# Building a graph's adjacency from a list of the pairs that hold edges, in place of four passes over all edge turns

## The reference

```python
dst = jnp.minimum((512 * jax.random.uniform(..., (16384,)) ** 2.0).astype(jnp.int32), 8191)
_o = jnp.argsort(dst, stable=True)          # the edges come sorted by destination
src, dst = src[_o], dst[_o]
A = A.at[src, dst].add(edge_weight)         # layer 0: weighted adjacency, then normalised
h = leaky_relu((A_norm @ h @ W_gcn[l] + b) @ W_mlp[l] + b)      # two rounds
# layer 1: four blocks of attention over the edges (edge counts)
# layer 2: adjacency of 0 and 1, made symmetric, three diffusion steps
# layer 3: two relations (edge_type 0 and 1), weights mixed from 30 bases:
w = jnp.einsum('rb,bio->rio', att, basis)   # basis is 30 x 512 x 512, per layer
```

## Time and profile before

| | |
|---|---|
| median of 3 runs | 1030.19 us (1028.79 to 1030.89) |
| the profiled execution: its own time | 1028.4 us |
| its span, first to last instruction | 1026.6 us |
| PE busy | 902.5 us, 88% of the span, 4358 instructions |
| DVE busy | 562.3 us, 55% |
| ACT busy | 429.2 us, 42% |
| POOL busy | 207.8 us, 20% |
| mean granted TensorE clock | 0.927 of full |
| adjacency: first opening of a bank to last closing | 12.7 to 188.6 us |

### The profile page before, as it was taken

One profiled execution on the slowest core, in us unless ns is written; L12 is line 12 of the kernel. 1 busy time (PEld: TensorE's weight loads), 2 busy tenths in 40 slices (PEclk: granted clock), 3 DMA queues, 4 the chain that ended last, 5 costly groups with the idle time before them and its releaser, 6 DMA issues.

```text
span 1026.6 us, 15204 instructions
## 1 busy us (share of the span) xinstructions
PE 902.5 (88%) x4358; PEld 685.6 (67%) x4359; DVE 562.3 (55%) x1236; ACT 429.2 (42%) x702; POOL 207.8 (20%) x147
## 2 busy tenths in 40 slices
PE   5878778799967999989999999999999796699998
PEld 4544354466745786967877778777878464678877
DVE  6845565885667545555565554664546847420110
ACT  4845465452332575236732477224662131221110
POOL 3000000230244012430133311332112322012100
PEclk9886986799987999999999999999999899599899
DMA  6727365445245444363454533552446653020100
GB/s 182 173 64 159 69 138 134 90 144 133 48 132 144 108 131 104 114 158 88 131 116 153 110 98 117 152 163 60 128 125 158 192 159 71 1 82 0 41 11 31
DMA packets 40920, 113.18 MB, mean 110 GB/s; under 512 B 9040, under 2 KB 9552, under 8 KB 33204
## 3 DMA queue, kind: packets, MB, share of 16 engines
q1 hardware_dynamic: 22116, 75.88, 31.3%
q10 hardware_dynamic: 18768, 36.83, 10.4%
HBM read 105.35 MB, written 7.34 MB: 110 GB/s over the span
## 4 chain that ended last, share of the span: by engine, by line
PE 71%; DVE 14%; issue 8%; ACT 4%; DVEq 2%; POOL 1%; ACTq 0%; DMA 0%
PE ring L1534 33%; PE ring L1772 21%; PE ring L1599 9%; PE ring L1552 5%; PE mix_ps L1563 1%; DVE stats L1018 1%; DVE yp L1327 1%; ACT yp L855 1%; PE mix_ps L1622 1%; DVE xl L1344 1%; ACT yp L886 1%; DVE yp L1332 1%; DVE y L1027 1%; DVE ohd L1143 1%; DVE mv L1021 1%
## 5 line engine op out<-in xcount | busy, mean ns | idle before, releaser
L632 POOL TENSOR_TENSOR wl<-wraw,wh 128x2048 fp32r<-128x2048 f32 x35 | 160.8, 4599 | 398.6 <-ACT wh L694 398.6
L1599 PE MATMUL ring<-ohs,ohd 128*128 128x512 f32 x368 | 101.0, 437 | 20.2 <-DVE ohs L1155 16.9
L1599 PEld LDWEIGHTS ring<-ohs,ohd 128*128 128x128 f32 x368 | 77.5, 215 | 49.4 <-DVE ohs L1155 26.3
L1143 DVE SCALAR_TENSOR_TENSOR ohd<-iota,dstT,vals 128x256 fp32r x184 | 79.7, 478 | 31.9 <-issue 26.0
L636 POOL TENSOR_TENSOR rstd<-ve,half 128x1 f32<-128x1 f32 x52 | 29.8, 576 | 291.2 <-DVE ve L1023 291.2
L737 ACT ACTIVATE ohs<-iota,minus_srcT 128x512 fp32r<-128x512 f32 x80 | 56.1, 716 | 45.3 <-PE ring L1599 20.7
L694 ACT ACTIVATE wh<-wraw 128x2048 fp32r<-128x2048 f32 x35 | 66.6, 1905 | 4.9 <-DMA wraw<-in_L_gnn_root 4.9
L1005 DVE TENSOR_TENSOR qk_l<-ring,qk_h 128x512 fp32r<-128x512 f32 x32 | 21.7, 690 | 75.8 <-ACT qk_h L719 75.8
L719 ACT ACTIVATE yT_h<-ring 128x512 fp32r<-128x512 f32 x32 | 19.1, 597 | 100.9 <-PE ring L1552 100.9
L1563 PE MATMUL mix_ps<-quad,att_shift 120*32 120x512 f32 x384 | 52.7, 634 | 3.3 <-ACT mixed L709 3.3
L1005 DVE TENSOR_TENSOR PT_l<-ring,PT_h 128x512 fp32r<-128x512 f32 x64 | 39.6, 681 | 19.6 <-ACT PT_h L719 19.6
(11 more groups left out here) (337 smaller groups left out, 2253.9 us busy)
## 6 DMA issues: line engine op xcount, KB each, us to landing
quad<-in_L_gnn_basis SPq DMA_DIRECT2D x60, 960.0 KB, 7.9
wraw<-in_L_gnn_m_w ACTq DMA_DIRECT2D x8, 1024.0 KB, 5.4
mix_scratch<-mixed SPq DMA_DIRECT2D x128, 32.0 KB, 1.8
wraw<-in_L_gnn_wv ACTq DMA_DIRECT2D x4, 1024.0 KB, 5.3
wraw<-in_L_gnn_wq ACTq DMA_DIRECT2D x4, 1024.0 KB, 5.2
wraw<-in_L_gnn_wk ACTq DMA_DIRECT2D x4, 1024.0 KB, 5.4
wraw<-in_L_gnn_wo ACTq DMA_DIRECT2D x4, 1024.0 KB, 5.4
wraw<-mix_scratch ACTq DMA_DIRECT2D x4, 1024.0 KB, 5.7
```

The lines of the kernel that those rows point to most:

```text
L632: g.tensor_tensor(wl[s][:], wraw[s][:], wh[s][:].bitcast(F32), ALU.subtract).then_inc(weight_lo, 1)
L1143: return v.scalar_tensor_tensor(out, at.unsqueeze(1).broadcast_to([P, 4, HALF]), dstT[:, e], vals[:, e, :].rearrange("p a b -> p (a b)").u ...
L1599: last = te.matmul(ring[:, bass.ds(banks[2 * r + j], 1), :], marks, ohs[:, u, :], start=False, stop=False)
```

## The change

The adjacency is no longer built in passes. On the chip a list is made of the pairs (turn, half) that hold edges, ordered by half, and one loop goes along it. `BODY` becomes 4, so a turn is 512 edges and there are 32; a pair is called a **unit**. The slots stay 8 (two units).

- **The list.** TensorE sums the flags of turns and halves (`unit_hit`), multiplies with triangles of ones for each unit's rank and whether it is the first of its half, and places codes of 6 bits, four to a word, in `words`. The chain is VectorE, TensorE, VectorE, TensorE, VectorE, about 20 short operations, on POOL's new constants (`upto`, `upto_half`, `unit_scale`); the 16 small `pow2` fills go.
- **The loop.** Each engine reads a word per four units (`value_load`), shifts out the turn and the "first of a half" bit, and does four tiles. The first 32 units are unconditional; behind them come up to 8 and then more, each behind a test of the count.
- **At a first unit** TensorE closes the two banks of the half before, opens two others, and ScalarE and VectorE move the closed half out after they made their tiles of the new unit.
- **Mixing.** One group stands ahead of every second unit (`j % 2 == 0`), starting ahead of unit 0; 16 groups in 32 units.
- **CT.** `CT[0] = Csum - CT[1]` moves from the end of each pass to the loop over H (round 0), behind each low part, and SP waits for these (`ct_ready`).
- **Norm.** The four `xn0` of VectorE become four operations on one column (`nmean`), and ScalarE computes `Relu(rstd * x + nmean)`.

```diff
-BODY = 8
-SPAN = 4
+BODY = 4
 TURNS = ET // BODY
-SLOTS = BODY
+SLOTS = 2 * BODY
-ACT_OF_ONE = (1, 3, 5, 7)
-ACT_OF_BOTH = (0, 2, 4, 6, 7)
+SURE = TURNS
+NEXT = SURE + 2 * WORD
+ACT_OF = (1, 3)
+EVICTS = 2
@@ SP
                 if g == 20:
-                    sp.wait_ge(pass_dve, DVE_EVICTS * (SETS_HELD + NT))
+                    sp.wait_ge(ct_ready, NT)
@@ ScalarE
+            def unit(i, j, word):
+                turn = act.snap((word >> (BITS * j)) & (TURNS - 1))
+                first = act.snap((word >> (BITS * j + BITS - 1)) & 1)
+                source_tiles(j % 2 * BODY, i * BODY, turn)
+                act.reg_add(half_no, half_no, first)
+                with act.If(first > 0):
+                    ...
+                    act.wait_ge(half_ready, done)
+                    evict(m, 0 or 1)
...
-                a.activation(xn0[:, t, :], xn0[:, t, :], ACT.Relu).then_inc(h0_hi, 1)
+                a.activation(xn0[:, t, :], x[:, t, :], ACT.Relu, bias=nmean[:, t:t + 1], scale=rstd[:, t:t + 1]).then_inc(h0_hi, 1)
@@ VectorE
+            def unit(i, j, word):
+                turn = dve.snap((word >> (BITS * j)) & (TURNS - 1))
+                first = dve.snap((word >> (BITS * j + BITS - 1)) & 1)
+                dve.reg_add(half_no, half_no, first)
+                half = dve.snap(half_no, min_val=0, max_val=HALVES - 1)
                 for u in range(BODY):
+                    s = j % 2 * BODY + u
+                    e = bass.ds(turn * BODY + u, 1)
+                    dve.wait_ge(onehot_used, i * BODY + (u + 1))
+                    ins = destination(half, s, e)
+                    if u not in ACT_OF:
+                        ins = v.tensor_scalar(ohs[:, s, :], iota[:], srcT[:, e], None, ALU.is_equal)
                     ins.then_inc(dst_ready, 1)
...
-                normalise(xn0[:, t, :], x[:, t, :], t, t)
+                dve.wait_ge(ln_rstd, t + 1)
+                v.scalar_tensor_tensor(nmean[:, t:t + 1], mv[:, t, 0:1], -1.0, rstd[:, t:t + 1], ALU.mult, ALU.mult).then_inc(ln_xn, 1)
...
                 v.tensor_tensor(hb_l[1][:, t, :], hv[:, t % 2, :], f(hb_h[1][:, t, :]), ALU.subtract).then_inc(tile_taken, 1)
+                v.tensor_tensor(CT[0][:, t, :], Csum[:, t, :], CT[1][:, t, :], ALU.subtract).then_inc(ct_ready, 1)
@@ TensorE
+            def unit(i, j, word):
+                first = pe.snap((word >> (BITS * j + BITS - 1)) & 1)
+                with pe.If(first > 0):
+                    done = pe.snap(half_no, min_val=0, max_val=HALVES - 1)
+                    ...
+                    zero(old[0], False)
+                    pe.wait_ge(half_act, done * EVICTS + EVICTS)
+                    zero(old[1], False).then_inc(half_ready, 1)
+                    pe.wait_ge(half_dve, done * EVICTS + EVICTS)
+                    zero(new[0], True)
+                    zero(new[1], True)
+                pe.reg_add(half_no, half_no, first)
+                ...
+                for u in range(BODY):
+                    s = j % 2 * BODY + u
+                    pe.wait_ge(dst_ready, i * BODY + (u + 1))
+                    if u in ACT_OF:
+                        pe.wait_ge(src_ready, i * BODY + (u + 1))
+                    for b in range(2):
+                        last = te.matmul(ring[:, banks[b], :], ohd[:, s, b, :], ohs[:, s, :], start=False, stop=False)
+                    last.then_inc(onehot_used, 1)
...
             with pe.Fori(0, NT) as m:
-                ...
+                for g in range(2):
+                    word = word_of(m * 2 + g)
+                    for j in range(WORD):
+                        if j % 2 == 0:
+                            mix_in_units(m, g * 2 + j // 2)
+                        unit(m * (2 * WORD) + (g * WORD + j), j, word)
```

More of the change, by code:

```diff
@@ L104, in sem @@
             return top.enter_context(nc.semaphore(name))
-        pre = Tiles(["tab", "flag"], 0, {"tab": 4, "flag": 5})
+        pre = Tiles(["tab", "flag", "rank", "words"], 0, {"tab": 4, "flag": 5, "rank": 6, "words": 5})
         mid = Tiles(["deg"], pre.end)
@@ L155, in program @@
         pace = sb("pace", [P, 64])
+        nmean = sb("nmean", [P, NT])
         nmin = sb("nmin", [P, 2, NT])
@@ new lines, in word_of, with later_units @@
+            def word_of(k):
+                return dve.value_load(words[0:1, bass.ds(k, 1)])
+            def later_units(k, count):
+                word = word_of(k)
+                for j in range(WORD):
+                    with dve.If(count > k * WORD + j):
+                        unit(k * WORD + j, j, word)
+            dve.wait_ge(flags_ready, 1)
+            with dve.Fori(0, SURE // WORD) as k:
+                word = word_of(k)
+                for j in range(WORD):
+                    unit(k * WORD + j, j, word)
@@ new lines, in _ @@
+            out = ring[:, pre.bank("flag"), :]
+            for c in range(2):
+                of = slice(c * (HALVES // 2), (c + 1) * (HALVES // 2))
+                te.matmul(out[:, 2 * c:2 * c + 2], turn_hit[:, of, :].rearrange("p m q -> p (m q)"), ones[:, 0:2], start=True, stop=True)
+            pe.wait_ge(table_ready, 8)
+            for c in range(2):
+                of = slice(c * (HALVES // 2), (c + 1) * (HALVES // 2))
+                last = te.matmul(out[:, 2 * c + 4:2 * c + 6], half_hit[:, of, :].rearrange("p m q -> p (m q)"), ones[:, 0:2], start=True, stop=True)
@@ new lines, in _ @@
+            pe.wait_ge(unit_step, 7)
+            out = ring[0:1, pre.bank("words"), :]
+            for c in range(2):
+                for j in range(WORD):
+                    te.matmul(out[:, 0:WORDS], unit_codes[:, c, j:j + 1], unit_at[:, c, j:UNITS:WORD], start=c + j == 0, stop=c == 1 and j == WORD - 1)
+            for c in range(2):
+                last = te.matmul(out[:, WORDS:WORDS + 1], unit_hit[:, c:c + 1], ones[:, 0:1], start=c == 0, stop=c == 1)
+            last.then_inc(tile_ready, 1)
@@ new lines, in word_of, with later_units, mix_in_units @@
+            def word_of(k):
+                return pe.value_load(words[0:1, bass.ds(k, 1)])
+            def later_units(k, count):
+                word = word_of(k)
+                for j in range(WORD):
+                    with pe.If(count > k * WORD + j):
+                        unit(k * WORD + j, j, word)
+            def mix_in_units(m, k):
+                if k == 0:
+                    pe.wait_ge(set_taken, m + 1)
+                pe.wait_ge(pass_loaded[k], m * 16 + 16)
+                for c in range(STRIPS):
+                    ins = te.matmul(mix_ps[c * STRIP:(c + 1) * STRIP, :],
+                                    att_shift[0:QUADS * BASES, 0, GROUPS - 1 - k:GROUPS - 1 - k + STRIP],
+                                    pass_quad(k)[:, c, :], start=k == 0, stop=k == GROUPS - 1)
+                ins.then_inc(quad_used, 1)
```

351 lines of the change are left out of this document (172 added, 179 removed).

## The result

The median fell from 1030.54 us (4 runs, 1028.79 to 1031.72) to 1003.10 us (4 runs, 1000.92 to 1005.52): a ratio of 0.9736, with a 95% interval from 0.9702 to 0.977. Forecast was 1021. The sign was right and the size was not: 27 us were gained, not 9. The profiled execution took 1000.92 us, its span 999.2, at a mean granted clock of 0.952 (before 0.927). It is one of two runs at 1000.9; the other two took 1005.3 and 1005.5 at 0.948 and 0.947, so the median lies midway.

The account below looks back on a forecast made before the run. TensorE was taken to carry most of the chain of waits, so what counts is when it gets work. Loop -19.1, after the loop -3.3, CT's wait +13.1 gave -9.3 us: 1021 us against the median, 8-in-10 range 1003 to 1038.

Parts of the forecast that it names:

- the loop on TensorE: TensorE's adjacency loop, from 37.4 us: terms sum to 132 us, last closing at 169.5 us, 19.1 us earlier than before.
- matmuls, cold start: In the loop: 312 matmuls at 0.245 us, 76.4 us, plus 2.4 us for a clock at 1.2 GHz after idling.
- mixing groups: In the loop: 16 mixing groups at 1.07 us and a little, 17.6 us.
- closings and openings: At seven changes of half: four bank openings or closings take 1.20 us each time, 8.4 us.
- borders 11.5, words 5, registers at 7 changes 4.9: TensorE idle: 0.5 us at 23 unit borders, 0.5 us for each of ten words, 0.7 us at each change of half.
- coupling and clock: In the loop: waits from buffers only two units deep and clock dips; 6 us, bounds 0 and 20.
- The start: Loop begins at 37.4 us, held by the first basis load, which hides the list's few us; later loads just hidden.
- After the loop: From last closing to transposes: statistics 2.65 us earlier, norm 0.65 us as POOL's hold moves to `angles`; 3.3 us saved.
- CT's wait: Between H and G: group (5, 1)'s load queues behind CT's stores; G 11.1 us later plus 2 slow, 13.1; bounds 9 and 17.
- The floor rival: Unit borders and word loads vanish behind queued matmuls, clock stays up: loop about 118, CT stall 11, total 1005 us; chance 0.22.
- Register work: Slower rival: each unit border costs 1.0 instead of 0.5 us, uncovered by mixing groups; about 1040 us; chance 0.20.
- no CT stall: Rival: SP or engines are faster than seen, or G doesn't need the load; -13, 1008 us; chance 0.08.

Follow-up runs that it names:

- The run with the late store: Changed kernel, but SP waits for CT and stores it only after the last of its 24 basis loads; measured 986.89 us, ratio to before 0.9578.

## Why the prediction was right or wrong

**The failed step: the loop on TensorE, 132 us against 113.8.** The terms, and what the groups of the profile after show for each:

| term | forecast | measured |
|---|---|---|
| matmuls, cold start | 78.8 | 80.2 |
| mixing groups | 17.6 | 18.0 |
| closings and openings | 8.4 | 9.1 |
| borders 11.5, words 5, registers at 7 changes 4.9 | 21.4 | 1.9 ("issue") |
| coupling and clock | 6 | 7.9 (waits for VectorE) |

The measured rows overlap by 3.3 us, which makes 113.8. The whole miss of 18 us, and a little more, is the fourth row: 21.4 us were charged and 1.9 were there. I priced each border at 0.5 us from idle rows of 0.25 and 0.79 us, of which only the first had "issue" as its releaser, and added word loads and registers as if TensorE stopped for each. In the profile after, sixteen matmuls with a border in them take 3.93 us. The run with six real operations more per unit shows why that is no free rule: the loop grew by 0.23 us a unit, some 0.15 of it without the clock. The present border lies below that edge.

**The work terms were right**, the cold start too (2.2 us in the first group and matmuls, forecast 2.4). The coupling came near in size (7.9 us of waits, 6 with the clock forecast), but not for the reason given: I had the depth of the buffers and the clock in mind, and 6.1 us of it are the seven changes of half; the clock did not dip inside the loop. The bound of VectorE and ScalarE at about 104 us was near: TensorE or VectorE relieved alone gave 1.0 and 2.4 us, all three together 10.7.

**The start** was right: 37.51 for 37.4 us, with the basis load as releaser after 16.9 us of nothing. The later loads were just hidden, as said: the fourth, issued at 32.4 us, landed after 20.4, at 52.8, and its group ran at 54.24.

**After the loop**, -3.8 us for -3.3: 2.9 from the earlier statistics (forecast 2.65), 0.9 from the norm (0.65). The hold stayed, as said, but its victim was the fourth `nmean` and not `angles`. By the rule that I cited (the Trainium skill, SBUF — State Buffer, section "SBUF: two separate sides"), VectorE's freed time is not gained while POOL's subtraction runs; the trace agrees, to the point that an operation on one column took 4.46 us beside it, and 0.16 without. But I cited it too widely: that section has the lock only for a VectorE operation in a two-port mode or with two inputs in SBUF (`nmean` has two), and `hb_l`, with one, was not held.

**CT's wait**: +12.2 us at the start of G (forecast 11.1) and 0.8 in G's slow first matmuls (forecast 2): 13.0 for 13.1. The run with the late store gave it back.

**The rivals.** The floor rival (loop 118, 1005 us, chance 0.22) is what happened. Its loop was 4 us too long and its CT stall 2 us too short, so that its total came within 2 us is partly luck. The result also lies at the very edge of my range of 1003 to 1038 us. Register work did not turn up at 1.0 us a border; "no CT stall" fell. The weights were wrong: against the floor I had only "two units of buffer", and no row.

## What to carry to other kernels

Price gaps between queued instructions by the rows in which such a gap lies inside a busy stretch, and by their releaser; a gap that the profile names "issue" after an idle stretch is no price for one behind queued work. When a wait is moved within an in-order queue, list what stands behind it: moving the small loads and two stores was worth 28 us, as much again as the whole change. Where engines hand a buffer round, as at the change of half, relieving each of them doesn't remove the wait; another order of the steps might, and was not tried. And an edit ahead of a looped block can move the block's time, here by 13.1 us a repeat: compare the stages that the edit did not touch.

## What the runs showed that I had not expected

- The same looped block of VectorE took 122.3 or 135.4 us a repeat, depending on 22 unrelated instructions ahead of it, with 21 or 36 packets in an instruction queue, idle of 4.96 and 3.04 us marked "issue" behind the jump back, and packets of that queue inside both.
- Four small strided transfers took 9.5 us to issue ahead of the loads, 26.4 us behind four loads of 960 KB, and 2.1 us in the middle of the loop.
- A VectorE operation on 128 x 1 elements took 4.46 us beside POOL's 4.51 us subtraction and 0.16 without it; one with an operand in PSUM kept its 0.69 us.
- Register operations that are only repeated additions are folded away: of 60 written, 16 were in the program. Count the instructions of an experiment before believing it.
